# Attention and mixture-of-experts kernel: the last two batches' chain in earlier slots, the sorting in small pieces, eight register loads in one

## What is computed

```python
x = x + xattn(layernorm(x), ctx, ctx, mask, Wq, Wk, Wv, Wo)      # 16 heads
h = layernorm(x)                                                 # (4096, 256)
scores = softmax(h @ gate_w.T)                                   # 8 experts
_, ids = top_k(scores, 2)
w = scores * one_hot(ids, 8).sum(axis=1)
g, u = split(einsum('nh,eih->nei', h, experts_gate_up))          # 352 each
out = einsum('neh,ne->nh', einsum('nei,ehi->neh', silu(g) * u, experts_down), w)
shared = (silu(h @ sg.T) * (h @ su.T)) @ sd.T                    # 704 wide
return x + out + sigmoid(h @ seg.T) * shared
```

## Time and profile before

| | |
|---|---|
| time, median of 3 runs | 837.18 us (831.12 to 838.23) |
| time of the profiled execution | 835.5 us |
| its span, first to last instruction | 833.6 us |
| TensorE busy | 747.2 us (90%) |
| VectorE busy | 551.4 us (66%) |
| ScalarE busy | 397.6 us (48%) |
| GpSimd busy | 335.1 us (40%) |
| mean granted clock of TensorE | 0.971 |

### The profile page before, as it was taken

How to read it: one execution, slowest core, us unless ns; L and a number is a source line. 1 busy time by engine, 2 the same in 40 slices (tenths; PEclk the granted TensorE clock), 3 DMA queues, 4 the chain that set the end, 5 groups by cost and what they waited for, 6 DMA issues and landing times.

```text
span 833.6 us, 22121 instructions
## 1 busy us (share of the span) xinstructions
PE 747.2 (90%) x8123; PEld 468.5 (56%) x8123; DVE 551.4 (66%) x1174; ACT 397.6 (48%) x679; POOL 335.1 (40%) x498
## 2 busy tenths in 40 slices
PE   3789898879897999999898979899999999999998
PEld 2444455445454555555445645567777777765555
DVE  5676676768888898888766677643333333348797
ACT  3225555445465556666564454244444444433232
POOL 5142144366648365445333134012121212247774
PEclk9979999899899999999999989999999999999999
DMA  4744555455554355454522123299989899754653
GB/s 135 201 143 141 161 162 141 121 168 152 142 164 146 116 150 157 132 145 125 175 87 81 24 90 108 65 160 165 177 162 167 162 165 173 149 144 128 227 153 113
DMA packets 164217, 118.25 MB, mean 142 GB/s; under 512 B 108434, under 2 KB 143506, under 8 KB 164116
## 3 DMA queue, kind: packets, MB, share of 16 engines
q1 hardware_dynamic: 146548, 82.44, 41.7%
q0 software_dynamic: 9552, 26.10, 10.3%
q10 hardware_dynamic: 8016, 8.33, 3.2%
HBM read 52.78 MB, written 38.14 MB: 109 GB/s over the span
## 4 chain that ended last, share of the span: by engine, by line
PE 54%; DVE 15%; DMA 10%; POOL 7%; issue 5%; ACT 4%; SPq 4%; ACTq 1%; DVEq 0%; POOLq 0%
PE ps_st L1828 15%; PE ps_m L1843 8%; PE ps_st L1422 7%; DVE mx L956 5%; PE ps_st L1064 4%; PE ps_o L1114 3%; PE ps_m L1138 3%; PE ps_o L1433 3%; POOL p L1570 3%; DMA arena<-ffn_dram 2%; PE ps_m L1204 2%; SPq L380 2%; DMA qk_scratch<-arena 2%; DMA sums<-odd 2%; PE ps_st L1082 2%
## 5 line engine op out<-in xcount | busy, mean ns | idle before, releaser
L956 DVE TENSOR_REDUCE mx<-ps_st 128x4 f32<-128x1024 f32 x128 | 155.6, 1217 | 30.2 <-PE ps_st L1082 22.3
L775 ACT ACTIVATE p<-ps_st 128x1024 f32<-128x1024 f32 x128 | 131.0, 1023 | 80.3 <-PE ps_st L1098 73.2
L1828 PE MATMUL ps_st<-fwh,p 128*128 x568 | 137.9, 312 | 1.6 <-DMA p<-expert_rows 1.6
L1562 POOL DMA_DIRECT2D sorted_out<-p x71 | 38.4, 541 | 181.3 <-ACT p L1619 177.6
L1828 PE MATMUL ps_st<-fwl,p 128*128 x284 | 88.8, 313 | 0.0
L1064 PE MATMUL ps_st<-maskq,identb 64*64 64x512 bf16 x512 | 54.1, 413 | 36.6 <-DVE mx L956 34.1
L1354 POOL DMA_INDIRECT expert_rows<-hrow,slot x64 | 64.7, 1011 | 45.1 <-DVE slot L1345 29.5
L1828 PEld LDWEIGHTS ps_st<-fwh,p 128*128 128x128 f16 x568 | 55.6, 98 | 28.4 <-issue 1.9
L1064 PE MATMUL ps_st<-mb_k,identb 64*64 64x512 bf16 x256 | 52.2, 404 | 14.6 <-ACT p L775 13.1
L1422 PE MATMUL ps_st<-q,arena 128*128 128x512 f16 x264 | 59.5, 379 | 1.7 <-DVE qk L1717 1.7
L1619 ACT ACTIVATE p<-ps_m 128x256 f32<-128x256 f32 x71 | 27.2, 383 | 70.5 <-PE ps_m L1843 67.6
(11 more groups left out here) (236 smaller groups left out, 1768.0 us busy)
## 6 DMA issues: line engine op xcount, KB each, us to landing
arena<-ffn_dram SPq DMA_DIRECT2D x20, 544.0 KB, 4.4
sorted_out<-p POOLq DMA_DIRECT2D x71, 128.0 KB, 3.0
qk_scratch<-arena SPq DMA_DIRECT2D x32, 256.0 KB, 2.6
qk<-qk_scratch SPq DMA_DIRECT2D x44, 128.0 KB, 2.9
xr<-x_dram SPq DMA_DIRECT2D x8, 512.0 KB, 4.6
arena<-ctx_dram SPq DMA_DIRECT2D x16, 256.0 KB, 3.2
hT_dram<-hT ACTq DMA_DIRECT2D x16, 256.0 KB, 2.8
out_dram<-xr SPq DMA_DIRECT2D x16, 256.0 KB, 3.0
```

Of the source, the lines that this page charges most:

```text
L775: eng.activation(expo[n % 4][:, :, :], ps_st[pair["T", n]][:, :].rearrange("p (h q) -> p h q", h=4), ACT.Exp, scale=SCALE).then_inc(s_e, 1)
L956: eng.tensor_reduce(mx[b % 2][:, qt, :].rearrange("p (h g j) -> p h g j", h=2, g=HG)[:, :, hg, :], ps_st[pair["S", 8 * b + n]][:, :].rearr ...
L1562: eng.dma_start(sorted_out[k * P:(k + 1) * P, :], ys[k % 3][:, :]).then_inc(r_st[k % 3], 16)
L1828: last = mm(o[:, 0:INTER], xgT[k % NXG][:, xl, dc, :], (fwh, fwl)[wl][:, bass.ds(e, 1), w0 + dc * INTER:w0 + (dc + 1) * INTER], start=dc = ...
```

## The change

There are five edits.

1. The table `tail` moves the steps of batches 13 to 15 up, by 1 slot (`o` of 14) to 4 slots (`ex`, `route` of 15), and `SKIP` loses slots 149 and 155, so that the filler ends in slot 159 instead of 161.
2. The last batch's division moves: the inversion to the start of slot 149, product and high half to slot 149 (from 153 and 154), low half to the start of slot 150 (from 154). On SP `shares_out` of batch 15 now stands ahead of its `join`.
3. `tables` is cut into 13 small pieces. Five of them stand in slot 160, behind `rk` (slot 158) and `combine_filler(4)` and ahead of the low half of the filler's last piece.
4. In step 6 of the shared expert one piece of the sorting stands behind each `hf` and one behind each low half, where a larger piece stood behind each low half only. `emap` comes with the first of them, `rowmap` with the fourth; two pieces remain for tiles 3 and 7.
5. TensorE's sequencer loads the experts of eight tiles with one instruction, without the check of bounds, before tiles 0, 8, ..., 64.

```diff
-        tail = {("rt", 13): 151, ("ex", 13): 152, ("route", 13): 153,
-                ("o", 14): 150, ("hn", 14): 151, ("rh", 14): 151, ("lo", 14): 152, ("ht", 14): 153, ("tw", 14): 154,
-                ("rt", 14): 154, ("ex", 14): 155, ("route", 14): 156,
-                ("o", 15): 155, ("hn", 15): 156, ("rh", 15): 156, ("lo", 15): 157, ("ht", 15): 158, ("tw", 15): 159,
-                ("rt", 15): 159, ("ex", 15): 160, ("route", 15): 160, ("rk", NB): 161}
+        tail = {("ht", 13): 149, ("tw", 13): 150, ("rt", 13): 150, ("ex", 13): 151, ("route", 13): 152,
+                ("o", 14): 149, ("hn", 14): 150, ("rh", 14): 151, ("lo", 14): 151, ("ht", 14): 153, ("tw", 14): 154,
+                ("rt", 14): 154, ("ex", 14): 154, ("route", 14): 154,
+                ("o", 15): 152, ("hn", 15): 153, ("rh", 15): 153, ("lo", 15): 154, ("ht", 15): 155, ("tw", 15): 156,
+                ("rt", 15): 156, ("ex", 15): 156, ("route", 15): 156, ("rk", NB): 158}
...
-            return usual + [(late, step) for n, step in enumerate((0, 1, 2, 3, 4, 6, 7)) if g == 8 * late + n]
+            return usual + [(late, step) for step in (6, 7) if g == 8 * late + 1]
...
-        FROM, SKIP = 8 * NB + LAG_S, (143, 149, 155)
+        FROM, SKIP = 8 * NB + LAG_S, (143,)
...
-                join(eng, b)
-                shares_out(eng, b)
+                if b < NB - LATE:
+                    join(eng, b)
+                    shares_out(eng, b)
+                else:
+                    shares_out(eng, b)
+                    join(eng, b)
...
+                    if 8 * i + u == LAST_T + 2:
+                        shares(NB - 1)
+                    if 8 * i + u == LAST_T + 3:
+                        low_share(NB - 1)
+                    if 8 * i + u == LAST_T + 13:
+                        for _ in range(5):
+                            next(moe.sorting)
                     if first:
                         shared_product(i, u)
...
                     eng.tensor_tensor(hf[k % 2][rows, :], up[k % 2][rows, :], gs[k % 2][rows, :], ALU.mult).then_inc(f_hf, 1)
+                    next(also, None)
...
-                experts[k] = e = eng.value_load(emap[0:1, k:k + 1], min_val=0, max_val=NE - 1)
+                if k % 8 == 0:
+                    n = min(8, NTILE - k)
+                    _, found = nc.values_load_multi_w_load_instructions(
+                        emap[0:1, k:k + n], engines=[mybir.EngineType.PE], min_val=0, max_val=NE - 1,
+                        skip_runtime_bounds_check_because="a sum of NE - 1 comparisons")
+                    experts.update(zip(range(k, k + n), found))
+                e = experts[k]
```

More of the change, by code:

```diff
@@ L908, in shared_product, with shares, low_share @@
                                              ALU.mult, ALU.mult).then_inc(moe.f_hf, 1)
+            moe.sorting = tables(eng, link, moe)
+            def shares(b):
+                eng.wait_ge(s_dr, 32 * (b + 1))
+                eng.reciprocal(den[:, :], den[:, :]).then_inc(s_rc, 1)
+            def low_share(b):
+                eng.wait_ge(s_onh, b + 1)
+                eng.tensor_tensor(onl[:, :, :], rb[:, :].rearrange("p (g t) -> p g t", g=HP), onh[:, :, :],
+                                  ALU.subtract).then_inc(s_onl, 1)
             def combine_filler(n):
@@ L1042, in _ @@
                             eng.tensor_tensor(rb[:, :], oj[:, :], rb[:, :], ALU.mult).then_inc(s_n, 1)
-                        if b >= NB - LATE and step == 7:
-                            eng.wait_ge(s_onh, b + 1)
-                            eng.tensor_tensor(onl[:, :, :], rb[:, :].rearrange("p (g t) -> p g t", g=HP), onh[:, :, :],
-                                              ALU.subtract).then_inc(s_onl, 1)
                         if step == 2:
-                            eng.wait_ge(s_dr, 32 * (b + 1))
-                            eng.reciprocal(den[:, :], den[:, :]).then_inc(s_rc, 1)
+                            shares(b)
                     if first:
@@ L1436, in shared_down, with lay_tables @@
     return last
+def lay_tables(moe):
+    carve, consts = moe.carve, moe.consts
+    moe.regions = consts[:, 0:NE]
+    moe.tile_starts = consts[:, 2 * NE:2 * NE + NT]
+    moe.tile_ids = consts[:, 2 * NE + NT:2 * NE + NT + NTILE]
+    moe.prod = carve(TOPK * NT * NE, FP32).rearrange("p (j n e) -> p j n e", j=TOPK, n=NT)
+    moe.cmp_ = carve(NE * NT, FP32)
+    moe.cross = carve(NTILE * (NE - 1), FP32, 1).rearrange("p (n e) -> p n e", n=NTILE)
+    moe.ends = [carve(NE, FP32) for i in range(2)]
+    moe.ntl = carve(NE, FP32)
+    moe.held = carve(NE, FP32)
+    moe.step_up = carve(NE, FP32)
+    moe.emapf = carve(NTILE, FP32, 1)
+    moe.emap = carve(NTILE, INT32, 1)
+    moe.rowsf = carve(NTILE, FP32, 1)
+    moe.rowmap = carve(NTILE, INT32, 1)
+    norm = moe.xn[:, :, :].rearrange("p t d -> p (t d)")
+    moe.all_slots, moe.shift, packed = (norm[:, TOPK * NT * i:TOPK * NT * (i + 1)].rearrange("p (j n) -> p j n", j=TOPK)
+                                        for i in range(3))
+    moe.packed = packed.bitcast(UINT32)
@@ L1736, in gathered @@
                 added[0] = n + 1
-            sorting = tables()
+            sorting = moe.sorting
             eng.wait_ge(moe.s_st, 8 * NB)
-            next(sorting)
             shared_gate(eng, link, moe, range(2 * TT * FILL - 2 * TT, NT))
```

112 lines of the change are left out of this document (53 added, 59 removed).

## The result

| | before | after |
|---|---|---|
| median of 20 executions each | 838.3 us | 832.15 us |
| their lowest and highest | 831.12 to 847.4 | 827.82 to 835.47 |
| profiled execution, its span | 835.5, 833.6 | 827.82, 826.0 |

The ratio is 0.9937, with a 95% interval from 0.9912 to 0.9961: some 5.3 us less, where the forecast was 1.0 us less. The ratio leaves out a kernel's slow runs, those over 1.5% above its fastest, so it says less than the 6.15 us between the two medians. So two things need an explanation: the 7.6 us between the two profiled spans, and the 5.3 us between the many executions.

What follows compares the result with a forecast made beforehand. TensorE was taken as the bound, full in the tiles, with 14.8 us at most to win at attention's end. The edits nearly cancel, 1 us won: 837.2 - 1.0 = 836.2 us, forecast's own range 834 to 839, eight in ten 831 to 841.

Steps and rivals of the forecast that it cites:

- Edit 2: Batch 15's shares: the 3.87 us wait before `o` goes, 4.8 us at `down(3)` replaces it; 1.7 to 1.9 us won there.
- Edit 1: Slot table: VectorE's queue makes `down(4)` wait 2.4 us, turning a lead of 1.8 us into a lag of 1.9.
- Edits 3 and 4: Sorting pieces cover VectorE's 2.1 us of waits in step 6, 7.6 us instead of 9.6; `down(6)` starts at 527.65.
- what is won here is what edit 1 lost: Step 6: small sorting pieces win back the 1.9 us lag from VectorE's queue; last low half at 527.6, as before.
- The clock: TensorE's clock may fall behind the new 2.4 us wait at `down(4)`: cost 0 to 1.8 us, half taken.
- Edit 5: TensorE's register loads in the tiles: single loads, 0.74 us at most, leave no idle array, so nothing is won.
- The rival of long loads: Loads of eight over some 0.9 us stop the array in the tiles: +1.4 to +7 us, chance 0.10.
- The rival of the chain that pays off: VectorE gets through slots 150 to 152 faster, the wait before `down(3)` shrinks: 4 to 8 us won, chance 0.13.
- The sum: Whole kernel: 1 us won, between 1.7 if the clock costs 0 and nothing if it costs 1.8.

Runs made afterwards that it cites:

- chain: The kernel before with only the new slot table and batch 15's earlier division and shares; median 838.6 us, ratio to before 1.0048.
- sort: The kernel before with only the sorting in small pieces, on the second chip; median 868.39 us, ratio to before 0.9958.
- single: The kernel after with single register loads instead of loads of eight, on the second chip; median 873.07 us, ratio to before 0.9935.
- single2: The kernel after with single register loads instead of loads of eight, again, on the third chip; median 837.82 us, ratio to before 1.0028.
- after2: The kernel after, unchanged, run again on the third chip; median 833.4 us, ratio to before 0.9954.
- ahead: The kernel after with product 11's low half put ahead of the ring's work on VectorE in slot 152; median 829.48 us, ratio to before 0.9948.
- same: A copy of the kernel before, nothing changed, on the first chip; median 838.51 us, ratio to before 1.005.
- loads: The kernel before with only the loads of eight expert numbers at a time on TensorE; median 832.79 us, ratio to before 0.9971.
- ahead2b: The kernel after with the low halves of products 11 and 14 put ahead in slots 152 and 156, third chip; median 824.85 us, ratio to before 0.9861.
- nop: The kernel before with one idle instruction ahead of all work on TensorE, ScalarE and VectorE, second chip; median 872.58 us, ratio to before 0.9991.
- ahead2: The kernel after with the low halves of products 11 and 14 put ahead in slots 152 and 156, second chip; median 862.43 us, ratio to before 0.9897.

## Why the prediction was right, and where its size was not

- **Edit 2** held nearly to the tenth. The untouched part ended 8.45 us earlier, so `o` of batch 15, forecast at 479.9, is to be looked for at 471.45: it started at 471.25, without a wait. The wait of 4.8 us foreseen at `down(3)` was 4.72, and 4.71 to 4.72 in each of the four other traces with this order.
- **Edit 1** held. The wait at `down(4)` was 2.10 us where 2.4 was foreseen. `chain` shows the lag on its own: the stretch with the schedule and without the small pieces is 2 us longer than before's.
- **Edits 3 and 4** held. VectorE's 2.1 us of waiting for ScalarE became 0.2, TensorE's wait at `down(6)` 1.73 (2.1 foreseen), and `down(6)` started at 519.82, that is 528.27 on before's time, against 527.65. The five pieces were priced at 3.0 us and took 3.4 (507.77 to 511.16). `sort` and `chain` show both halves of "what is won here is what edit 1 lost": -2.3 and +2 us against the mean of before's order.
- **The clock** was bounded by 0 and 1.8 us at `down(4)` and half was taken. In the profiled execution of after it cost nothing there, and `down(6)` took 3.9 us. That was luck: in the four other traces with this order (`chain`, `single`, `single2`, `after2`) the clock fell behind the same wait of 2.1 us, and `down(4)` took 5.5 us from first to last matmul for 3.8. Here are `down(4)` in after and most of it in `after2`, with the granted clock third from the end:

```profile
499.30:503.20 3.90, 3.90 (x36) 3.51 (x37) 1.29 (x2) 0.63 (x1) 2.84 (x3) 1.00 0.29 103
503.80:507.10 3.30, 3.30 (x17) 2.33 (x16) 0.96 (x2) 0.63 (x1) 2.45 (x3) 0.50 0.25 84
```

  At `down(3)` the clock cost more than foreseen in the profiled execution (6.32 us; at full clock, in `ahead`, 3.67), and in the others with this order `down(3)` took 5.1 to 5.8. With it the stretch came out 1.1 us shorter in the first pair of traces. Over all traces: 57.9, 57.5, 57.7, 58.3 and 58.0 with before's order, 56.8, 57.3, 57.7 and 57.2 with after's, so 0.6 us shorter in the mean, forecast 1.0.
- **Edit 5 is the term that was mis-sized**, the step that says: "even with 0.74 the array is never idle in the tiles. So nothing is won by fewer loads." The row was right and the inference was not (the load of 0.74 us began 2.2 us ahead of the array). It took the longest of 71 loads in one execution for the longest there is. In other executions the same loads reach 1.0 us, often at every second tile for a long way. The tile loops with single loads were 203.7, 203.4, 203.7, 206.0, 212.6, 211.7 and 208.5 us, 207.1 in the mean; with loads of eight 204.1, 203.2, 204.2, 203.8, 204.4 and 203.4, 203.8 in the mean. That is 3.2 us (the means mix three chips, and the two longest loops are from the second), and `after2` against `single2` on one chip gives 4.1 in all. On the first chip none of the three loads over 0.9 us (one in `same`, two in `chain`) left a gap, so there the gain of `loads` is not traced to it. The prediction even had the price, a load "over some 0.9 us", and applied it to the new loads only. As `chain` shows, it holds where the load begins only some 0.9 us ahead of the array.
- **The rival of long loads** fell: eight numbers take 0.60 us. Here the Trainium skill, page "Runtime: NRT & Kernel Launch", section "Instruction fetch mechanics", gives about 200 ns for each register, and the page speaks of registers loaded from HBM; here the numbers lie in SBUF. The measured 0.59 to 0.61 us for eight are 75 ns for each, and the measurement decides. Two of the nine loads were longer in all six traces: the first, 0.78 us, and the last, of seven numbers, 1.07 to 1.08. The last began 2.2 us ahead of the array each time, and the profile puts what idle time stood at its tile (none in `ahead2b`, 0.8 us in `after2`) down to the tile's data.
- **The rival of the chain that pays off** did not come true in after (its `down(3)` waited the full 4.7 us). But its price, 4 to 8 us, was about right: where `ahead2b` removes the waits and the clock holds, 8.3 us are won in the stretch against `after2`.
- **The sum.** Measured against before: -5.3, and -3.8 in `after2`'s ratio. Of that edit 5 brings 3 to 4 us by the tile loops, edits 1 to 4 some 0.6 to 1 by the stretches. The times of edits 1 to 4 alone settle nothing: `single` has a ratio of 0.9935, `single2` of 1.0028. What is left is below the 0.5% by which two copies of one program differed. So most of what was won came from the one edit that was priced at nothing, and that the median fell inside the range, 1.2 us above its lower end, was in good part luck: its lower end had been set by the chain that pays off and by the fastest run of before, and not by this edit.

What stays open: why single loads are 0.3 us in one execution and 1.0 in the next, and why the clock and the waits of the first 470 us differ by 7 to 8 us between executions of one program. No run was made on either.

## What to carry to other kernels

A cost that lies on a sequencer just below what the array is fed ahead looks free in a trace where it stays below; ask how far it is from the edge, and double it in an experiment before pricing it at nothing. The spread of many executions is a hint and no proof: here the standard deviation was 1.2 to 3.4 us with loads of eight and 3.9 to 6.3 with single ones, but 2.8 in `chain` and 3.5 in `sort`, which have single loads too. When a schedule is moved up, list for each consumer what stands ahead of its input in the feeding engine's queue: here two low halves that stood behind less urgent work cost 8 us, more than the whole change brought. And measure a copy of the kernel beside it before believing half a per cent.

## What the hardware showed that I had not expected

- A register load on TensorE's sequencer took 0.30 us or up to 1.06 us for the same instruction; with its arithmetic it holds the queue some 0.35 us longer than its own duration. Loading eight at once took 0.60 us. A load of 1.04 us cost nothing where it began 2.2 us ahead of the array (`chain`), and one of 1.02 us cost 0.5 us where it began 0.96 us ahead (`single2`).
- Behind a wait of 4.7 us the granted clock had fallen each time (`down(3)` in 5.1 to 6.3 us for 3.7). Behind one and the same wait of 2.1 us it held once and fell four times; behind 2.58 us in `ahead` it fell, behind 2.27 us in `ahead2` it held. In `ahead2b`, with no wait above 1.8 us in the stretch, it stayed at 1.00. So between 2.1 and 2.6 us the length of the wait does not tell. The lower clock is TensorE's 1.2 GHz level, against 2.4.
- One of three chips ran the same program in 872 us where the others took 835 to 838. In `nop`'s trace TensorE stood still again and again after 770 us, for 0.4 to 1.2 us with no releaser in the profile (`issue`), and the part behind the tiles took 118 us for 97. The three other traces of that chip are alike (117 to 119 us). The routing product of batch 13 comes at 483 to 486 us there, for 467 to 475 on the others, while the loop with loads of eight is as long as elsewhere (203.8 us in `ahead2`). No run looked for the cause:

```profile
777.38 1.00 issue
778.39 0.39 PE ps_o L1436
778.78 1.03 issue
779.81 0.40 PE ps_o L1436
```
